# Rows of the first mixture gathered by token number, and grouped-query projections begun on half of the tokens

## Chip, cores and metric

The kernel runs on one core of one Trainium2 chip. The metric is the device time of one launch in microseconds (us); lower is better. TensorE (PE in the profile) multiplies matrices and turns tiles, VectorE (DVE), ScalarE (ACT) and GpSimd (POOL) do the elementwise work, and SyncE (SP) issues most of the DMA transfers; gathers and scatters by index are issued from POOL's queue.

## The reference

A two-layer decoder on x of 4 x 256 tokens x 256 channels. Each part normalises x and adds its result to x:

```python
x = x + L0_attn(layernorm(x))     # a linear-decay mixer
x = x + L0_xattn(layernorm(x))    # latent cross attention over 1601 context rows
x = x + L0_ffn(layernorm(x))      # the first mixture: top-1 of 8 experts, capacity 160
x = x + L1_attn(layernorm(x))     # grouped-query attention, 16 heads, 4 key/value heads
x = x + L1_xattn(layernorm(x))
x = x + L1_ffn(layernorm(x))      # the second mixture: top-2 of 16 experts, one shared
```

The first mixture, as far as it matters here:

```python
logits = tokens @ gate_weight.T                  # (1024, 8)
top1 = argmax(logits);  mask = one_hot(top1, E)
ranks = cumsum(mask, axis=0) - 1                 # place of a token in its expert's queue
mask = mask * (ranks < C)                        # C = 160 places per expert
dispatch = einsum('tec,th->ech', sec_mask, tokens)
expert_out = gelu(dispatch @ w1) @ w2            # per expert
out = einsum('tec,ech->th', combine_weights, expert_out)
```

And the start of the grouped-query attention:

```python
q, k, v = split(x @ w_qkv.T)                     # 16 + 4 + 4 heads of 128
q, k = layernorm(q) , layernorm(k)               # per head, with gain and bias
q = q * cos + rotate_half(q) * sin               # k likewise
```

## The kernel before

The 1024 tokens are 8 tiles of 128 rows; a half is four tiles, and X (128 x 8 x 256) stays in SBUF for the whole kernel. Every engine has one program, written out in the order in which it is to run. PSUM has eight banks, handed out in turn by `PsumBanks`: `begin` on TensorE claims the next bank for a key and waits until the engine named for it has emptied the key eight places back; `turn` transposes up to four tiles of 128 x 128 into one bank. `copy_out` on ScalarE or VectorE waits for a bank to be filled and copies it to SBUF. `link` makes an engine wait for its own last result.

**Normalising.** `normalise(k, g)` on VectorE adds the part before to X for the four tiles of half g, takes statistics, waits for ScalarE's square root (`deviations(k, g)`), and writes HN[k] with four operations (L1481), each counted in `hn_ready`. `turn_x(k)` on TensorE waits for `hn_ready` and turns a half into two banks, ("ht", k, g, 0) and ("ht", k, g, 1); one is copied out by ScalarE and one by VectorE into HT[k].

**The first mixture.** After the attention output product of token tiles 6 and 7 (`attended`), TensorE turns the second half of HN[2] (`turn_half(1)`), makes the router's logits (`logits0`, 16 matmuls of 8 columns a half), turns the weights of the next stage in between (`qkv_weights`, from a_nat, and then `awo`, from a_wo), and counts ranks with a triangle of ones (`rank0`). VectorE makes the slot number of each token, expert times 160 plus rank, into f_idx (L1728; a token without a place gets a number beyond the last slot), and then centres the weights a_wT of queries and keys (`centre`, four times a reduction, a small operation and a subtraction over 1280 columns, L1752 to L1754). Meanwhile:

- POOL clears f_xg, 128 x 10 x 256 (L2080), and f_yg (L2082). SP writes the cleared f_xg over all 1280 rows of xs0 in HBM (L2225).
- When f_idx is there, POOL scatters the eight tiles of HN[2] into the rows of xs0 (L2087, eight indirect transfers of 128 KB, `rows_sent`).
- When all eight have landed, SP loads xs0 back into f_xg, in five transfers of two slot tiles (L2230, `rows_back[g]`).
- TensorE turns group g (`slots_turned`, four transposes into a bank, key ("xg", g)); the even groups are copied out by ScalarE, the odd ones by VectorE. NEXT0 puts the groups before the experts: groups 0 and 1 before expert 0, group 2 before expert 2, 3 before 3, 4 before 5. `up0(e)` and `down0(e)` are the expert's two products, with Gelu on ScalarE between; VectorE copies the result (f_y), and SP stores it to ys0.
- When all results are stored, POOL gathers them back by token (f_yg, L2094, eight indirect transfers), and `normalise(3, g)` adds them to X (`result`, L1760).

SP issues its DMAs in the order of its program; before the tables of the next stage (a_cos, L2220, to a_gb) it waits for tile 7 of the attention output. Then come the zeros for xs0 and the experts' weights f_w1 and f_w2 (L2226, L2227, 2 MB each). In POOL's program the head tables of the next stage stand between the scatters and the gathers of results.

**The grouped-query projections.** After `turn_x(3)` all engines meet in `ended(3)`. Then TensorE runs units n: `qkv(n)` for token tile t = n // 6 and 512 columns g = n % 6 (four records of a matmul of 512 columns each in the trace); g = 5 is the values. For each of the 40 query and key units ScalarE squares (L1345), VectorE makes the rotated parts and sums the squares (`parts`, L1801 to L1804), ScalarE takes a square root (L1348) and scales four heads (L1336), POOL adds the parts (`rotated`, L2101) and the bias (`biased`, L2107), and TensorE turns the result (`qk_turn`), for unit n - 4 after unit n. POOL's order is rotated 0, 1, 2, biased 0, rotated 3, biased 1, and so on. The causal mask is loaded by SP after `ended(3)`.

The second mixture, at the end of the kernel, already fetches its rows by token number. It holds the operations that the change adds to the first, on twice as many places: VectorE, L1905 to L1923 (e_idx, e_q, e_one, e_A, e_B, e_ids); TensorE, `tile_tokens`.

## Time and profile before

| | us |
|---|---|
| median of the runs | 1380.8 (1380.19 to 1387.83, 3 runs) |
| the profiled execution | 1383.64, of which the span from first to last instruction 1381.8 |
| granted TensorE clock, mean | 0.952 of 2.4 GHz |
| TensorE busy | 1269.7 (92%) |
| VectorE busy | 869.0 (63%) |
| GpSimd busy | 823.2 (60%) |
| ScalarE busy | 632.4 (46%) |

Busy time is a share of the whole span; the kernel is a row of stages with different limits, so what an edit in one stage is worth has to be read in that stage. All times in the rows count from the start of the span. A clock of 1.00 is 2.4 GHz, 0.50 is 1.2 GHz. A row of a timeline merges neighbouring instructions of the same kind; the brackets at its end give the idle time before it and what ended it.

### The profile page before, as it was taken

The page shows a single profiled execution, that of the slowest core. Times are in us where ns is not written, and L with a number is a line of the kernel's source. Part 1 is how long each engine was busy: PE and PEld are TensorE (multiplying, and loading weights), DVE is VectorE, ACT ScalarE, POOL GpSimd, SP SyncE. Part 2 cuts the span into 40 slices and gives each one's busy share as a digit, 9 for nine tenths or more (in the row PEclk, how much of TensorE's full clock was granted, in tenths as well). Part 3 has the DMA queues.
Part 4 walks back from the last instruction along what each step waited for, and adds up shares of the span by engine and source line. Part 5 has one row for each costly group of instructions (what it writes and reads, how often), then busy time and mean ns, then how long its engine had stood idle before and what let it go on. Part 6 is the DMA issues. An engine that isn't in the chain of part 4 may idle for free.

```text
span 1381.8 us, 20338 instructions
## 1 busy us (share of the span) xinstructions
PE 1269.7 (92%) x7115; PEld 826.3 (60%) x7115; DVE 869.0 (63%) x1484; ACT 632.4 (46%) x1684; POOL 823.2 (60%) x747
## 2 busy tenths in 40 slices
PE   7999997999999999999999567998999999998792
PEld 4865554666666666666668553445776884557582
DVE  4756666677777777778865526675666113764543
ACT  3731123445544455444551315887666015881151
POOL 1267005799999999999993535887544003660444
PEclk9999997999999999999999688998999997998996
DMA  8501111000000000000004720000000105200263
GB/s 260 134 9 34 36 31 27 9 8 9 9 12 8 9 9 9 12 9 9 9 5 166 234 60 12 1 0 1 1 1 1 28 1 155 62 1 32 67 144 118
DMA packets 67532, 60.12 MB, mean 44 GB/s; under 512 B 19440, under 2 KB 64392, under 8 KB 66920
## 3 DMA queue, kind: packets, MB, share of 16 engines
q1 hardware_dynamic: 64408, 50.56, 13.1%
q0 software_dynamic: 3024, 8.26, 2.6%
q8 instruction: 58, 0.95, 0.3%
q14 instruction: 42, 0.34, 0.1%
HBM read 40.58 MB, written 9.83 MB: 36 GB/s over the span
## 4 chain that ended last, share of the span: by engine, by line
PE 79%; DVE 6%; ACT 5%; POOL 5%; issue 4%; DMA 1%; DVEq 0%; SPq 0%; POOLq 0%; ACTq 0%
PE PS L503 73%; PE PS L511 5%; ACT s_sc L1379 2%; POOL a_m L2107 2%; POOL a_m L2101 2%; DVE s_mx L1826 1%; ACT a_m L1336 1%; DVE pm L1599 1%; DVE HN L1481 1%; POOL slot_rows L2087 1%; PE PS L717 0%; POOL s_sc L2122 0%; PE PS L673 0%; PE PS L611 0%; DVE stats L1471 0%
## 5 line engine op out<-in xcount | busy, mean ns | idle before, releaser
L2047 POOL TENSOR_TENSOR PWS<-PWS 128x1024 f32<-128x1024 f32 x160 | 379.5, 2372 | 45.6 <-ACT PWS L1264 26.2
L1599 DVE TENSOR_REDUCE pm<-PS 128x2 f32<-128x1024 f32 x192 | 225.8, 1218 | 69.5 <-PE PS L503 69.1
L1264 ACT ACTIVATE PWS<-PS 128x512 f32<-128x512 f32 (+1 forms) x416 | 213.1, 600 | 78.5 <-PE PS L503 77.2
L503 PE MATMUL PS<-PWS,KVR 128*64 128x256 f32 (+1 forms) x1664 | 185.9, 380 | 0.0
L503 PE MATMUL PS<-QALL,KH 128*128 128x512 f32 (+1 forms) x416 | 182.9, 440 | 0.9 <-DVE QM L1623 0.9
L503 PE MATMUL PS<-QM,KL 68*128 68x512 f32 (+1 forms) x416 | 167.1, 402 | 0.0
L2122 POOL TENSOR_SCALAR s_sc<-s_sc,s_ri 128x128 f32<-128x128 f32 (+1 forms) x256 | 103.9, 425 | 99.5 <-DVE s_ri L1833 99.5
L503 PEld LDWEIGHTS PS<-PWS,KVR 128*64 128x64 f32 (+1 forms) x1664 | 121.1, 137 | 59.3 <-issue 0.9
L503 PEld LDWEIGHTS PS<-QALL,KH 128*128 128x128 f32 (+1 forms) x416 | 77.9, 187 | 76.9 <-ACT PWS L1264 57.2
L1379 ACT ACTIVATE s_sc<-PS,s_nb 128x128 f32<-128x128 f32 (+1 forms) x256 | 104.4, 431 | 4.9 <-DVE s_nb L1829 4.9
L1826 DVE TENSOR_REDUCE s_mx<-PS 128x2 f32<-128x512 f32 (+2 forms) x112 | 65.7, 611 | 52.0 <-PE PS L503 51.7
L503 PE MATMUL PS<-KH,QALL 64*128 64x512 f32 (+1 forms) x512 | 89.3, 408 | 7.0 <-DVE pm L1599 7.0
L503 PE MATMUL PS<-a_wT,HT 128*128 128x512 f32 x192 | 90.1, 602 | 0.7 <-ACTq L490 0.7
L1275 ACT ACTIVATE QALL<-CTX 128x256 fp32r<-128x256 f32 x32 | 13.3, 417 | 154.3 <-DVE CTX L1636 154.3
L503 PEld LDWEIGHTS PS<-QM,KL 68*128 68x128 f32 (+1 forms) x416 | 79.0, 190 | 6.2
L503 PEld LDWEIGHTS PS<-KH,QALL 64*128 64x128 f32 (+1 forms) x512 | 46.9, 189 | 43.6 <-issue 26.0
L503 PE MATMUL PS<-z_HTh,z_w 128*128 128x512 f32 x192 | 67.5, 420 | 2.4 <-DVEq L490 2.4
L2150 POOL DMA_INDIRECT e_x<-token_rows,e_ids x31 | 29.4, 949 | 64.4 <-DVE e_ids L1923 45.7
L1249 ACT ACTIVATE QALL<-PS 64x512 fp32r<-64x512 f32 x32 | 18.9, 592 | 106.4 <-PE PS L503 106.0
L2101 POOL TENSOR_TENSOR a_m<-a_m,a_m 128x512 f32<-128x512 f32 x40 | 50.8, 1271 | 27.0 <-DVE a_m L1803 27.0
L1502 DVE TENSOR_TENSOR X<-X,PS 128x256 f32<-128x256 f32 x40 | 16.7, 418 | 76.6 <-PE PS L503 76.6
L1367 ACT ACTIVATE s_pt<-PS 128x512 f32<-128x512 f32 x64 | 38.5, 602 | 50.1 <-PE PS L511 50.1
(319 smaller groups left out, 2516.9 us busy)
## 6 DMA issues: line engine op xcount, KB each, us to landing
QALL<-qlo SPq DMA_DIRECT2D x32, 128.0 KB, 2.4
QM<-QALL SPq DMA_DIRECT2D x64, 64.0 KB, 2.0
f_w<-in_L_ffn_w_dram SPq DMA_DIRECT2D x2, 2048.0 KB
tile_results<-e_y SPq DMA_DIRECT2D x31, 128.0 KB
a_nat<-in_L_attn_w_qkv_dram SPq DMA_DIRECT2D x1, 3072.0 KB, 13.4
x_wq<-in_L_xattn_Wq_dram SPq DMA_DIRECT2D x1, 2048.0 KB, 11.2
x_wo<-in_L_xattn_Wo_dram SPq DMA_DIRECT2D x2, 1024.0 KB, 6.8
a_wo<-in_L_attn_w_o_dram SPq DMA_DIRECT2D x1, 2048.0 KB, 17.8
```

The costliest lines, as they stand in the source:

```text
L503: return nc.tensor.matmul(o, a, b, start=start, stop=stop, **kw)
L511: last = nc.tensor.transpose(ps[0:w, c:c + r], a, ident[0:r, 0:r])
L1264: nc.scalar.activation(PW[c][0:rows, j * HALF:(j + 1) * HALF], st_bank("block", LT * u + lt)[0:rows, :], ACT.Exp).then_inc(p_ready, 1)
L1367: nc.scalar.activation(s_pt[:, m % 2, 0, :], ps, ACT.Copy).then_inc(emptied["act_turned"], 1)
L1379: ins = nc.scalar.activation(s_sc[:, k % 4, h, 0:nk], ps[:, j * nk:(j + 1) * nk], ACT.Exp, bias=s_nb[:, k % 3, h:h + 1], scale=scale, accu ...
L1599: V.tensor_reduce(pm[u % 2][:, :, i // 3, i % 3], src, AX, ALU.max).then_inc(nat_read, 1)
L1826: ins = V.tensor_reduce(s_mx[:, k % 3, i * per:(i + 1) * per], banks.bank(key)[:, 0:per * nk].rearrange("p (h k) -> p h k", h=per), AX, AL ...
L2047: G.tensor_tensor(ACC[:, :], PW[0][:, :] if i == 0 else ACC[:, :], PW[i + 1][:, :], ALU.add).then_inc(acc_step, 1)
L2101: G.tensor_tensor(a_m1[:, n % 6, :], a_m1[:, n % 6, :], a_m2[:, n % 2, :], ALU.add).then_inc(m_sum, 1)
L2107: G.tensor_tensor(m1, m1, a_bt[:, i, s, :].unsqueeze(1).to_broadcast([P, 4, P]), ALU.add).then_inc(qk_ready, 1)
L2122: ins = G.tensor_scalar(s_sc[:, n % 4, h, 0:nk], s_sc[:, n % 4, h, 0:nk], s_ri[:, n % 4, h:h + 1], 1.0, ALU.mult, ALU.mult)
L2150: G.indirect_dma_start(e_x[:, j % 8, :], None, xs1, IndirectOffsetOnAxis(ap=e_ids[:, j:j + 1], axis=0)).then_inc(tile_back[j % 8], 16)
```

## The change

1. **Rows by token number.** HN[2] is stored as it is, by two transfers of SP, one for each half (`rows_stored`); xs0 now has 1024 rows. The clear of f_xg, the zeros over xs0 and the eight scatters are gone. VectorE splits each slot number into place (modulo 128) and tile, makes one-hots of both (f_B; f_A holds the tile's one-hot times the token's number within its tile and times 128 times its tile), eight bf16 matmuls multiply them on TensorE (key "ids0", placed after four of the six turns of `qkv_weights(1)`), and VectorE adds the two parts to f_ids: the token of each slot. POOL gathers ten tiles of 128 rows by f_ids straight into f_xg; `rows_back[g]` counts two gathers. A slot without a token fetches token 0, whose result nobody reads.
2. **All five groups** ("xg", g) are copied out by ScalarE.
3. **Projections on half of the tokens.** TensorE turns only the first half before the projections, and the second after unit 4; `qkv` waits for the banks of its own half. The ended(3) of all engines is gone, and the later ones are renumbered. VectorE copies ("ht", 3, 0, 0) between its two normalisations; ScalarE copies both banks of the second half, after its work for unit 1. The mask load waits for the last of these copies.
4. On SP the store of the first half stands before the wait for tile 7, the store of the second, with a wait for its HN[2], before the loads of the tables; the constants f_c are a fourth load ahead of a_nat.

```diff
+        xs0 = nc.dram_tensor("token_rows_3", [B * T, C], F32, kind="Internal").ap()
+        f_B = at("f_B", 190720, [P, NT, P], BF16)
+        f_A = at("f_A", 57344, [P, NT, 2, TILES0], BF16)
@@ turn_x (TensorE)
-                        turn(("ht", k, g, kc), "act" if kc and k != 1 or (k, g) in ((0, 0), (5, 0)) else "dve",
+                        turn(("ht", k, g, kc), "act" if kc and k != 1 or (k, g) in ((0, 0), (3, 1), (5, 0)) else "dve",
@@ slots_turned (TensorE)
-                pe.wait_ge(rows_back[g], 16)
-                turn(("xg", g), "dve" if g % 2 else "act",
+                pe.wait_ge(rows_back[g], 32)
+                turn(("xg", g), "act",
@@ tensor
             rank0()
-            qkv_weights(1)
+            qkv_weights(1, range(0, 4))
+            pe.wait_ge(slot_onehot, 1)
+            ps = begin("ids0", "dve")
+            for t in range(NT):
+                last = mm(ps[:, 0:2 * TILES0], f_B[:, t, :], f_A[:, t, :, :].rearrange("p s j -> p (s j)"), t == 0, t == NT - 1)
+            last.then_inc(filled, 1)
+            qkv_weights(1, range(4, 6))
...
-            turn_x(3)
-            ended(pe, 3)
+            turn_x(3, (0,))
...
             def qkv(n):
                 t, g = n // 6, n % 6
+                if g == 0 and t % 4 == 0:
+                    for kc in range(KC):
+                        pe.wait_ge(*banks.emptied(("ht", 3, t // 4, kc)))
...
                 qkv(n)
                 t, g = n // 6, n % 6
+                if n == 4:
+                    turn_x(3, (1,))
                 if g < 5 and 5 * t + g >= 4:
                     qk_turn(5 * t + g - 4)
@@ scalar
-            for g in range(2):
-                deviations(3, g)
-            ht_out(3)
-            ended(act, 3)
+            deviations(3, 0)
+            heads_out(3, 0, 1)
+            deviations(3, 1)
...
                     copy_out(("qkv", n // 5 - 1, 5), a_v[:, n // 5 - 1, :])
+                if n == 1:
+                    for kc in range(KC):
+                        heads_out(3, 1, kc)
                 if n >= 4:
                     qk_out(n - 4)
@@ vector
             V.tensor_copy(f_idx[:, :], f_slot[:, :]).then_inc(slots_ready, 1)
+            dve.wait_ge(slots_ready, 1)
+            link(V.tensor_scalar(f_qu[:, :], f_idx[:, :], P - 1, None, ALU.bitwise_and))
+            link(V.tensor_copy(f_q[:, :], f_qu[:, :]))
+            link(V.tensor_tensor(f_jq[:, :], f_slot[:, :], f_q[:, :], ALU.subtract))
+            link(V.tensor_tensor(f_one[:, :, :], bcast(f_jq[:, :], TILES0), f_tiles.unsqueeze(1).to_broadcast([P, NT, TILES0]), ALU.is_equal))
+            V.tensor_scalar(f_A[:, :, 0, :], f_one[:, :, :], f_p, None, ALU.mult)
+            V.tensor_tensor(f_A[:, :, 1, :], f_one[:, :, :], bcast(f_high, TILES0), ALU.mult)
+            V.tensor_tensor(f_B[:, :, :], bcast(f_q[:, :], P), f_iota.unsqueeze(1).to_broadcast([P, NT, P]),
+                            ALU.is_equal).then_inc(slot_onehot, 1)
+            ps = banks.take("ids0", "dve")
+            dve.wait_ge(*banks.filled("ids0"))
+            V.tensor_reduce(f_idf[:, :], ps[:, 0:2 * TILES0].rearrange("p (s j) -> p j s", s=2), AX, ALU.add).then_inc(emptied["dve"], 1)
+            dve.wait_ge(*banks.emptied("ids0"))
+            V.tensor_copy(f_ids[:, :], f_idf[:, :]).then_inc(slot_ids, 1)
...
             normalise(3, 0, result)
+            copy_out(("ht", 3, 0, 0), HT[3][:, 0, 0:HALF])
             normalise(3, 1, result)
-            ht_out(3)
-            ended(dve, 3)
@@ gpsimd
-            G.memset(f_xg[:, :, :], 0.0)
             pool.drain().then_inc(slots_cleared, 1)
             link(G.memset(f_yg[:, :, :], 0.0))
             last_slot = G.to_reg(SLOTS0 - 1)
-            pool.wait_ge(slots_zeroed, 16)
-            pool.wait_ge(slots_ready, 1)
-            for t in range(NT):
-                G.indirect_dma_start(xs0, IndirectOffsetOnAxis(ap=f_idx[:, t:t + 1], axis=0), HN[2][:, t, :], None,
-                                     bounds_check=last_slot, oob_is_err=False).then_inc(rows_sent, 16)
+            pool.wait_ge(rows_sent, 32)
+            pool.wait_ge(slot_ids, 1)
+            for j in range(TILES0):
+                G.indirect_dma_start(f_xg[:, j, :], None, xs0, IndirectOffsetOnAxis(ap=f_ids[:, j:j + 1], axis=0)).then_inc(rows_back[j // 2], 16)
@@ sync
+            sp.dma_start(f_c[:, 0:209], tri_c[:, P:P + 209]).then_inc(moe0_loaded, 16)
...
+            rows_stored(0)
             sp.wait_ge(*banks.emptied(("xo", NT - 1)))
+            rows_stored(1)
...
-            sp.wait_ge(slots_cleared, 1)
-            sp.dma_start(xs0.rearrange("(j p) c -> p j c", p=P), f_xg[:, :, :]).then_inc(slots_zeroed, 16)
...
-            sp.wait_ge(rows_sent, 16 * NT)
-            for g in range(SLOTS0 // P // 2):
-                sp.dma_start(f_xg[:, 2 * g:2 * g + 2, :],
-                             xs0[2 * g * P:2 * (g + 1) * P, :].rearrange("(j p) c -> p j c", p=P)).then_inc(rows_back[g], 16)
...
-            sp.wait_ge(phase_ended, 4 * 3)
+            sp.wait_ge(*banks.emptied(("ht", 3, 1, 1)))
```

## Rows read from the trace of the kernel before

**Rows 1.** Windows by stage: length, busy time by engine, clock, DMA share, GB/s.
```profile
778.00:790.00 12.00, 0.03 (x1) 0.04 (x1) 6.64 (x7) 1.09 (x3) 9.42 (x13) 0.61 0.44 149
```

**Rows 2.** TensorE's timeline: start us, us, instruction, count, idle time before and releaser.
```profile
755.54 1.84 PE L503 MATMUL PS<-g_T,HT 128*128 128x8 f32 x16
...
761.51 1.09 PE L511 MATMUL PS<-ident,HN 128*128 128x128 f32 x8 [2.33 <-DVE HN L1481]
763.39 3.44 PE L503 MATMUL PS<-g_T,HT 128*128 128x8 f32 x16 [0.79 <-ACT HT L1145]
...
789.97 1.97 PE L511 MATMUL PS<-ident,f_xg 128*128 128x128 f32 x8 [11.98 <-DMA f_xg<-slot_rows]
...
796.96 0.60 PE L511 MATMUL PS<-ident,f_xg 128*128 128x128 f32 x4
...
830.62 1.97 PE L511 MATMUL PS<-ident,HN 128*128 128x128 f32 x8 [13.57 <-DVE HN L1481]
...
838.95 10.36 PE L503 MATMUL PS<-a_wT,HT 128*128 128x512 f32 x20 [0.72 <-ACTq L490]
851.02 0.66 PE L511 MATMUL PS<-ident,a_m 128*128 128x128 f32 x4 [1.72 <-POOL a_m L2107]
```

**Rows 3.** VectorE's timeline, first mixture and start of the projections.
```profile
757.48 3.98 DVE L1481 TENSOR_SCALAR HN<-X,mv,rstd 128x256 f32<-128x256 f32 x4
...
771.27 0.17 DVE L1728 CAST f_idx<-f_slot 128x8 uint32<-128x8 f32 x1
...
773.60 1.49 DVE L1754 TENSOR_TENSOR a_wT<-a_wT,a_mu 128x1280 f32<-128x1280 f32 x1
...
834.82 1.38 DVE L1481 TENSOR_SCALAR HN<-X,mv,rstd 128x256 f32<-128x256 f32 x4
...
847.06 0.66 DVE L1801 TENSOR_TENSOR a_m<-PS,a_gc 128x512 f32<-128x512 f32 x1
```

**Rows 4.** GpSimd's timeline, first mixture: the two clears and three of eight scatters.
```profile
756.49 2.23 POOL L2080 MEMSET f_xg<- 128x2560 f32 x1
758.86 1.80 POOL L2082 MEMSET f_yg<- 128x2048 f32 x1 [0.15 <-issue]
772.33 1.20 POOL L2087 DMA_INDIRECT slot_rows<-HN,f_idx  x1 [11.67 <-DVE f_idx L1728]
773.84 2.12 POOL L2087 DMA_INDIRECT slot_rows<-HN,f_idx  x1 [0.31 <-issue]
...
777.55 1.64 POOL L2087 DMA_INDIRECT slot_rows<-HN,f_idx  x1 [0.30 <-issue]
```

**Rows 5.** SP's timeline: tables, expert weights, and the rows' way back.
```profile
756.19 0.34 SPq L2220 DMA_DIRECT2D a_cos<-in_cos_c_dram  x1
...
759.87 0.72 SPq L2226 DMA_DIRECT2D f_w<-in_L_ffn_w_dram  x1
...
787.15 2.41 SPq L2230 DMA_DIRECT2D f_xg<-slot_rows  x5
```

**Rows 6.** Windows of 1 us, first, one within and last of the full DMA stream (columns as above).
```profile
763.00:764.00 1.00, 0.61 (x4) 0.64 (x4) 0.52 (x4) 0.29 (x1) 0.00 (x0) 0.76 0.84 295
...
769.00:770.00 1.00, 1.00 (x6) 1.00 (x7) 0.01 (x1) 0.98 (x2) 0.00 (x0) 0.50 1.09 349
...
779.00:780.00 1.00, 0.00 (x0) 0.00 (x0) 0.96 (x2) 0.10 (x1) 0.70 (x2) 1.00 0.84 306
```

**Rows 7.** VectorE's timeline in the second mixture: from slots to one-hots.
```profile
1282.34 0.17 DVE L1905 CAST e_idx<-e_slot 128x16 uint32<-128x16 f32 x1
...
1284.77 2.35 DVE L1913 TENSOR_TENSOR e_B<-e_q,e_c 128x1024 bf16<-128x1024 f32 x2
```

**Rows 8.** The tile f_yg: its gathers (ns min/median/max, first and last start), and their landing.
```profile
L2094 POOL DMA_INDIRECT f_yg<-slot_results,f_idx x8: 994/998/1072, 820.6 to 829.8; - x8
...
DMA to landing us min/median/max: 2.8/2.8/2.9
```

**Rows 9.** ScalarE's timeline: the first square of the projections.
```profile
842.53 0.60 ACT L1345 ACTIVATE a_sq<-PS 128x512 f32<-128x512 f32 x1 [3.68 <-PE PS L503]
```

More of the change, by code:

```diff
@@ L330, in decoder @@
         slots_cleared = sem("slot_rows_cleared")
-        slots_zeroed = sem("slot_rows_zeroed")
         slots_ready = sem("token_slots_ready")
-        rows_sent = sem("token_rows_sent")
+        slot_onehot = sem("first_slot_one_hots_ready")
+        slot_ids = sem("slot_tokens_ready")
+        rows_sent = sem("token_rows_stored_3")
         res_added = sem("token_results_added")
@@ L915, in _ @@
                 qk_turn(n)
-            ended(pe, 4)
+            ended(pe, 3)
             def softmax_units(tag, units, turnable, score, use):
@@ L988, in _ @@
             turn_x(4)
-            ended(pe, 5)
+            ended(pe, 4)
             for ct in range(KC):
@@ L1128, in _ @@
                 shared_down(t)
-            ended(pe, 6)
+            ended(pe, 5)
         @block.scalar
@@ L1353, in _ @@
                     copy_out(("qkv", n // 5 - 1, 5), a_v[:, n // 5 - 1, :])
+                if n == 1:
+                    for kc in range(KC):
+                        heads_out(3, 1, kc)
                 if n >= 4:
                     qk_out(n - 4)
-            ended(act, 4)
+            ended(act, 3)
             def softmax_units(tag, units, base_n, scale):
@@ L1396, in _ @@
             turned_norm(4)
-            ended(act, 5)
+            ended(act, 4)
             for ct in range(KC):
@@ L1444, in _ @@
             nc.scalar.activation(f_e[:, :, :], f_e[:, :, :], ACT.Exp).then_inc(e_exp, 1)
-            ended(act, 6)
+            ended(act, 5)
         @block.vector
@@ L1767, in _ @@
             for e in range(E0 + 1):
-                for g in NEXT0[e] if e < E0 else ():
-                    if g % 2:
-                        copy_out(("xg", g), f_xT[:, :, 2 * g * P:2 * (g + 1) * P], lambda ps: ps.rearrange("p (k s) -> p k s", k=KC))
                 if e >= 1:
@@ L1816, in _ @@
             V.tensor_copy(s_identb[:, :], ident[:, :]).then_inc(mask_set, 1)
-            ended(dve, 4)
+            ended(dve, 3)
             def softmax_units(tag, units, base_n, scale, after):
@@ L1847, in _ @@
             turned_norm(4, added("ao"))
-            ended(dve, 5)
+            ended(dve, 4)
             def y_after(n, unit):
@@ L1960, in _ @@
                 V.scalar_tensor_tensor(X[:, t, :], e_yg[:, t, 1, :], e_w[:, 1, t:t + 1], X[:, t, :], ALU.mult, ALU.add).then_inc(x_final, 1)
-            ended(dve, 6)
+            ended(dve, 5)
         @block.gpsimd
@@ L2095, in _ @@
                                      bounds_check=last_slot, oob_is_err=False).then_inc(res_back[t], 16)
-            ended(pool, 3)
             def rotated(n):
@@ L2113, in _ @@
                     biased(n - 2)
-            ended(pool, 4)
+            ended(pool, 3)
             G.memset(y_v[:, :, :, :, :], 0.0).then_inc(v_cleared, 1)
@@ L2137, in _ @@
             masked_keys(0)
-            ended(pool, 5)
+            ended(pool, 4)
             masked_keys(1)
@@ L2155, in _ @@
                     G.indirect_dma_start(e_yg[:, t, k, :], None, ys1, IndirectOffsetOnAxis(ap=e_idx[:, k * NT + t:k * NT + t + 1], axis=0)).then_inc(both_back[t], 16)
-            ended(pool, 6)
+            ended(pool, 5)
         @block.sync
```

23 lines of the change are left out of this document (17 added, 6 removed).

## Prediction, made before the changed kernel was run

> **What bounds the kernel now.** I read the windows by stage first, then the chain of waits from 750 to 860 us, and then the timeline of each engine around the two places that the change touches. The page has TensorE busy for 92% of the span, but from 778 to 790 us it does nothing (0.03 of 12 us) [rows 1]. There it waits 11.98 us for rows of the first mixture [rows 2], and the timelines say why: slot numbers stand at 771.44 (771.27 + 0.17), eight scatters through POOL's queue follow, then a copy back from HBM at 787.15 [rows 3 to 5]. A second gap of 13.57 us ends at 830.62, when the first half of the tokens is normalised, and the second half follows before the projections start at 838.95 [rows 2]. So two places carry the change: the way of the rows (771 to 790), and the start of the projections (830 to 851). What lies between them moves along.
>
> **The head start from the removed clear.** The clear of f_xg (2.23 us) and that of f_yg (1.80) run on POOL from 756.49 to 760.66 [rows 4]. The four HN operations of VectorE between them take 3.98 us, the same four at 834.82 only 1.38 [rows 3]: the ones that meet a clear end with it. Without the f_xg clear, the f_yg clear runs from about 756.7 to 758.5, the first HN operation ends with it, three more of about 0.35 follow, and the second half is ready at about 759.7 in place of 761.46. That is 1.8 us off the chain. TensorE then idles 0.5 us instead of 2.33 before the transposes at 761.51. The 16 router matmuls on that half take 3.44 us, the 16 on the first half took 1.84 [rows 2]; the granted clock falls inside 763 to 764 [rows 6], after that gap. The new matmuls run from about 761.6 to 763.5, with hardly a gap before them, so I take them at 2.4 GHz and 1.84 us: 1.6 us more. Both ends: 0 and 1.6. Slot numbers: 771.44 - 1.8 - 1.6 = 768.0.
>
> **The new work between slots and rows.** The before shows the same operations in its second mixture: from e_idx at 1282.34 to the end of the two e_B operations at 1287.12 (1284.77 + 2.35) [rows 7]. Here there are half the slots: the small ones 0.21 each with their link, the 80-element one-hots 0.2 to 0.27, one e_B of 1.22 in place of two. Three times 0.21, 0.27, 0.15, 0.2 and 1.22 are 2.5 us. Eight matmuls, TensorE's answer and the semaphore: 0.6. Reduction and cast: two small operations like the cast to e_idx (0.17) with their links, 0.46 [rows 7]. POOL's start after the last value took 0.89 in the before (771.44 to 772.33). First gather at 768.0 + 2.5 + 0.6 + 0.46 + 0.89 = 772.5, nearly where the first scatter stands now, since the head start pays for the one-hots.
>
> TensorE has to be free for those eight matmuls at 770.6: before them lie rank0, which ended at about 770.0 and now ends 3.4 earlier, and 16 transposes (0.2 each at the slow clock), so it is free by 769.8. Behind them it has 40 transposes left (1.97 us for 8 cold ones: at most 10 us), done by 781, before the rows come. ACT copies them out meanwhile. VectorE's centring of a_wT (4 times about 3.3 us) starts only after the ids, at 772, and ends at 785; its next work, the copy of the first f_y, comes at about 788. Hidden.
>
> **Rows by gather.** TensorE's first expert needs xg 0 and, because both groups are turned before it, xg 1: four gathers. Alone a gather takes 0.99 us (f_yg) plus 0.3 between two, and lands 2.8 us after its start [rows 8]. But the issues at 773.84 and 777.55 took 2.12 and 1.64 us [rows 4]; each met a TENSOR_TENSOR of the centring, which runs from 773.60 for 1.49 us and again every 3.25 us [rows 3]. The centring is behind the ids by nearly as much as the gathers, so the pattern stays: in the before the fourth issue ended 779.19 - 772.33 = 6.9 us after the first began. So the fourth ends at 779.4 and lands 1.8 us later, at 781.2. Unheld, the fourth would start 3.9 us after the first and land at 779.2. Against 789.97 that is 8.8 us. The first group was turned meanwhile: of the 8 transposes only 4 (0.9 us of the 1.97) are left. Together 9.7 us up to the end of the experts. The gathers for groups 2 to 4 come every 2.6 to 3.4 us, TensorE asks for the first of them at 796.96, 7 us after its start [rows 2], and for the others about 3 and 9 us after that: hidden. That ACT now copies all five groups costs nothing: an expert takes TensorE about 3 us, and ACT spends on it one copy of 0.6 at most and the Gelu. Head tables start 3 us later on POOL, and have ten to spare.
>
> The Trainium skill says otherwise on one point: SBUF — State Buffer, "Who interferes with whom", says that a VectorE tensor_tensor with both inputs in SBUF locks out GpSimd's reads, and infers that generating descriptors for a GpSimd DMA, which needs the write side, is not held up. The trace of this case shows issues prolonged by about the rest of the TENSOR_TENSOR. By the page the fourth gather would land 2.0 us earlier, and the sum would be 1367.6.
>
> **The expert weights** must be there too. SP now waits for the second half before it issues a_cos, where it began at 756.19, so f_w1 goes from 759.87 [rows 5] to 759.7 + 0.5 + 3.2 = 763.4, 3.5 us later. The DMA engines are full from 763 to 779.8 [rows 6], by the tiles' sizes with 1.3 MB of zeros and 4.2 MB of weights and six scatters; at 349 KB per us the zeros cost 3.8 us, and they are gone. The stream ends about where it did, near 780; the first expert asks at 782.1. Hidden, with 2 us to spare. The store of the first 0.5 MB at 746 delays a_wo by 1.5 us, and TensorE asks for it only at 757.24; bound 0 to 1.
>
> **Projections.** Shown in the times of the before, everything after TensorE's experts unchanged up to 830.62: 8 transposes (1.97) and the ACT copy (0.7) give qkv(0) at 833.3 instead of 838.95, 5.6 us early. But this is not the gain. The second half's transposes stand behind five units on TensorE, and ACT copies them out (heads_out(3, 1)) after square 1 and before square 2. Five units took 10.36 us in the before [rows 2], with a cold start; from 833.3 that is 843.6, a little less because the transposes have begun to warm it: 843.3. Then 8 transposes (1.0, half of the cold 1.97), the ACT copy and square 2 (0.6 each, [rows 9]): VectorE starts its third unit at 845.6 instead of 847.06 [rows 3]. From there to the first qk_turn at 851.02 [rows 2] the sequence is the old one (POOL adds in the order r2, b0). Gain 1.5 us. VectorE's copy of ht 3,0,0 before normalise(3, 1) delays the second half by about 1.8 us to 838.0: not late, TensorE turns at 843. Ends: 3.2 us if all five units run at 2.4 GHz, 0 if the cold part doubles. The 119 us after that have POOL and the PSUM order as before; I price them at 0. The barrier, the drain and the mask load: 0, nothing waits on them last.
>
> **Sum.** 9.7 + 1.5 = 11.2 us. Against the profiled span 1381.8 (its run 1383.6) that is 1370.6; against the median 1380.8 of the runs, 1369.6. One per cent, about what a measurement of this kernel can tell, is 13.8 us.
>
> **Rivals.**
> 1. *The gathers are not held, and the projections start warm*: 2.0 + 1.7 more, 1365.9, over 1% faster. For it: the phase of the centring to the gathers can slip by a microsecond. Against: two of the first four issues met it. The page's inference above is the first half of this rival.
> 2. *Rows or weights late in the full DMA stream*: the gathers run at 772 to 779 under the stream of weights. The worst a queue can do is to serve them after it: 780 + 0.5 MB at 349 = 781.5, and the later landing for the last 1.8: 783.3; with a cold router (1.6) and no gain at the projections: 11.2 - 2.1 - 1.6 - 1.5 = 6.0, so 1374.8.
> 3. *Gathers far slower than the f_yg ones* (the other side): the four rows' transfers come from HBM while weights stream; no row shows that. Price: each us of landing is one us. At 11.2 us, a landing at 792.4, it turns slower than before; over 1% from 806. The stream is over at 780, so this needs a new cause.
> 4. *The overlap gives its full 5 us* (ACT not behind TensorE): 1366.1. Against: the order in the code.
>
> DMA: Bandwidth & Descriptors ("Queues, rings and completion order") of the Trainium skill says each DMA engine takes turns between queues by packets. No row of the before shows a gather's landing under load; by that rule the gathers would come before the stream's end, as in my sum.
>
> **Numbers.** Forecast 0.60; rival 1 0.10, rival 2 0.18, rival 3 0.04, rival 4 0.08. Predicted 1369.6. The range takes in rivals 1, 2 and 4 and a little of the runs' own spread: 1364.5 to 1376. Over 1% faster (below 1367.0) needs rival 1 or 4: 0.18. Slower by over 1%: half of rival 3, 0.02. Within: 0.80.
>
> **What would show it.** Second half of HN 2 ready 1.8 us earlier, router matmuls of 1.8 us, first gather near 772.5, first expert matmul near 782, experts' end near 807; then in the first projections an ACT gap before the third square, ended by TensorE's transposes. It would be wrong if the clock falls all the same, if TensorE waits for weights, or if the tile period in the projections is no longer 14.1 us.

## Result and profile after

| | before | changed |
|---|---|---|
| median of 20 runs, us | 1381.25 (1375.34 to 1392.67) | 1374.33 (1366.67 to 1388.71) |
| ratio, with its 95% interval | | 0.9937 [0.9919, 0.9955] |
| span of the profiled execution | 1381.8 | 1379.6 |
| mean granted clock | 0.952 | 0.954 |

The ratio is 8.7 us less (6.2 to 11.2), the medians differ by 6.9. The ratio leaves out three slow executions of the changed kernel (1387.65 to 1388.71) and none of the kernel before, so it flatters the change a little: over all 20 of each the means differ by 6.6 us. Forecast were 1369.6 in a range of 1364.5 to 1376 and no change over 1%. Range and class came out, but the time lies near that of the second rival (1374.8), and partly by its mechanism, as the rows show.

At the end of stage 2 the changed kernel's profile is 0.25 us ahead (the last addition to X on VectorE at 755.49, before 755.74), in code that the change does not touch. That is taken off below. VectorE and GpSimd, from the removed clear to the gathers, answer to [rows 3, 4]:

```profile
756.45 1.81 POOL L2114 MEMSET f_yg<- 128x2048 f32 x1 [0.15 <-issue]
...
757.23 2.14 DVE L1504 TENSOR_SCALAR HN<-X,mv,rstd 128x256 f32<-128x256 f32 x4
...
770.96 0.17 DVE L1765 CAST f_ids<-f_idf 128x10 uint32<-128x10 f32 x1
...
773.29 1.49 DVE L1791 TENSOR_TENSOR a_wT<-a_wT,a_mu 128x1280 f32<-128x1280 f32 x1
774.82 1.49 DVE L1789 TENSOR_REDUCE a_mu<-a_wT 128x10 f32<-128x1280 f32 x1
```

HN takes 2.14 us in place of 3.98, and the token numbers stand at 771.13. The chain of waits then runs from them to the rows (start, us, what):

```profile
772.00 1.17 POOL f_xg L2119
...
773.48 2.13 POOL f_xg L2119
...
775.91 0.95 POOL f_xg L2119
...
777.16 6.37 DMA f_xg<-token_rows,f_ids
```

The first gather stands at 772.00 (forecast 772.5). The second starts beside the TENSOR_TENSOR at 773.29 and is held to 2.13 us; the third starts beside the TENSOR_REDUCE at 774.82 and takes 0.95. The fourth, the last that the first expert needs, lands 6.37 us after its start, at 783.54; the forecast was 781.2. SP's timeline and, in a second fence, windows of 1 us say what was in the DMA engines [rows 5, 6]:

```profile
763.35 0.44 SPq L2263 DMA_DIRECT2D f_w<-in_L_ffn_w_dram  x1
763.83 6.42 SPq L2264 DMA_DIRECT2D f_w<-in_L_ffn_w_dram  x1
```

```profile
763.00:764.00 1.00, 1.00 (x8) 1.00 (x9) 0.64 (x4) 0.01 (x1) 0.00 (x0) 0.66 0.19 56
...
766.00:767.00 1.00, 1.00 (x7) 1.00 (x7) 0.55 (x3) 0.99 (x2) 0.00 (x0) 0.50 0.18 51
...
769.00:770.00 1.00, 0.76 (x4) 0.35 (x2) 1.00 (x3) 0.75 (x2) 0.00 (x0) 0.50 1.00 354
...
780.00:781.00 1.00, 0.39 (x2) 0.39 (x3) 1.00 (x1) 0.00 (x0) 0.69 (x2) 0.69 1.00 329
781.00:782.00 1.00, 0.73 (x4) 0.33 (x2) 0.97 (x2) 0.23 (x1) 1.00 (x1) 0.50 0.55 192
```

The weights were issued at 763.35 as forecast (763.4), but the engines moved 51 to 56 KB a us until 767 and were full only later, up to 781: the stream ends between 781 and 782, some 1.7 us behind that of before. The four gathers are issued under it, and the fourth lands 2 us after its end. TensorE's timeline, which answers to [rows 2]:

```profile
759.42 1.09 PE L523 MATMUL PS<-ident,HN 128*128 128x128 f32 x8 [0.49 <-DVE HN L1504]
761.30 1.92 PE L515 MATMUL PS<-g_T,HT 128*128 128x8 f32 x16 [0.79 <-ACT HT L1167]
...
780.61 1.12 PE L523 MATMUL PS<-ident,f_xg 128*128 128x128 f32 x4 [5.48 <-DMA f_xg<-token_rows,f_ids]
783.58 1.11 PE L523 MATMUL PS<-ident,f_xg 128*128 128x128 f32 x4 [1.85 <-DMA f_xg<-token_rows,f_ids]
784.49 3.68 PE L515 MATMUL PS<-f_xT,f_w 128*128 128x160 f32 x16
...
823.30 1.97 PE L523 MATMUL PS<-ident,HN 128*128 128x128 f32 x8 [13.48 <-DVE HN L1504]
826.00 11.60 PE L515 MATMUL PS<-a_wT,HT 128*128 128x512 f32 x20 [0.73 <-issue]
837.44 1.04 PE L523 MATMUL PS<-ident,HN 128*128 128x128 f32 x8
843.72 1.12 PE L523 MATMUL PS<-ident,a_m 128*128 128x128 f32 x4 [5.25 <-POOL a_m L2137]
844.63 5.61 PE L515 MATMUL PS<-a_wT,HT 128*128 128x512 f32 x8
850.07 0.60 PE L523 MATMUL PS<-ident,a_m 128*128 128x128 f32 x4
```

The wait of 11.98 us has become two of 5.48 and 1.85, with transposes at half speed between them. The first half of the normalised tokens is turned at 823.30 in place of 830.62. Then the gain shrinks: before the first turn of queries TensorE stands for 5.25 us (1.72 before), and the eight matmuls behind it take 5.61 us in place of 3.60, so that the second turn of queries follows the first after 6.35 us in place of 3.93. The rows of the kernel before for that:

```profile
851.52 3.60 PE L503 MATMUL PS<-a_wT,HT 128*128 128x512 f32 x8
854.95 0.60 PE L511 MATMUL PS<-ident,a_m 128*128 128x128 f32 x4
```

ScalarE and VectorE of the changed kernel show what it waited for [rows 3, 9]:

```profile
838.07 1.08 ACT L1167 ACTIVATE HT<-PS 128x512 f32<-128x512 f32 x2 [4.80 <-PE PS L523]
839.04 0.60 ACT L1365 ACTIVATE a_sq<-PS 128x512 f32<-128x512 f32 x1
...
839.74 0.69 DVE L1834 TENSOR_TENSOR a_m<-PS,a_gc 128x512 f32<-128x512 f32 x1 [4.52 <-issue]
```

ScalarE idles 4.80 us for the transposes of the second half, copies them, and only then squares the third unit. VectorE starts that unit at 839.74, which is 16.44 us after the turn at 823.30; before it was 847.06 - 830.62 = 16.44 too.

### The profile page after: what moved, and what is told of

It reads as the page before. It is cut to its first block, busy times and chain, and to the rows that moved or that the text cites. A ratio compares the mean times of both kernels' runs of the same rounds, so it can differ in the third digit from the quotient of the medians.

```text
span 1379.6 us, 20358 instructions
## 1 busy us (share of the span) xinstructions
PE 1272.7 (92%) x7123; PEld 826.8 (60%) x7123; DVE 868.2 (63%) x1490; ACT 634.6 (46%) x1687; POOL 824.0 (60%) x748
## 4 chain that ended last, share of the span: by engine, by line
PE 79%; DVE 6%; ACT 5%; POOL 4%; issue 4%; DMA 1%; DVEq 0%; SPq 0%; POOLq 0%; ACTq 0%
PE PS L515 73%; PE PS L523 5%; ACT s_sc L1402 2%; POOL a_m L2137 2%; POOL a_m L2131 2%; DVE s_mx L1859 1%; ACT a_m L1356 1%; DVE pm L1622 1%; DVE HN L1504 0%; PE PS L729 0%; DMA f_xg<-token_rows,f_ids 0%; POOL s_sc L2152 0%; PE PS L685 0%; POOL f_xg L2119 0%; PE PS L623 0%
## 5 line engine op out<-in xcount | busy, mean ns | idle before, releaser
L1622 DVE TENSOR_REDUCE pm<-PS 128x2 f32<-128x1024 f32 x192 | 225.8, 1218 | 69.3 <-PE PS L515 68.7
L515 PE MATMUL PS<-a_wT,HT 128*128 128x512 f32 x192 | 93.4, 620 | 0.7 <-issue 0.7
```

The source lines that it names most:

```text
L515: return nc.tensor.matmul(o, a, b, start=start, stop=stop, **kw)
L1622: V.tensor_reduce(pm[u % 2][:, :, i // 3, i % 3], src, AX, ALU.max).then_inc(nat_read, 1)
```

## How the profiles are compared

Executions of one kernel spread over up to 22 us (1366.67 to 1388.71), so I split every profiled span at four rows: the last addition to X before HN 2 is normalised (the end of stage 2); **R**, from there to the turn of the first half of HN 3 on TensorE (first mixture); **P**, from that turn to the second turn of queries (start of the projections); **L**, from the addition to the turn of HN 4's second half (it holds R, P and the rest of the attention); **Y**, from there to the router matmuls of the second mixture (latent attention); and the rest. For the kernel before, the rows give L = 1141.62 - 755.74 = 385.88 and Y = 1263.35 - 1141.62 = 121.73:

```profile
755.74 0.42 DVE L1502 TENSOR_TENSOR X<-X,PS 128x256 f32<-128x256 f32 x1 [2.35 <-PE PS L503]
...
1141.62 1.27 PE L511 MATMUL PS<-ident,HN 128*128 128x128 f32 x8 [2.34 <-DVE HN L1481]
...
1263.35 1.93 PE L503 MATMUL PS<-m_rT,HT 128*128 128x16 f32 x16 [1.40 <-ACT HT L1145]
```

All values are differences of such rows. "chip" numbers the three groups of kernels that ran on one chip.

| kernel | chip | addition at | R | P | L | Y | rest |
|---|---|---|---|---|---|---|---|
| before | - | 755.7 | 74.9 | 24.3 | 385.9 | 121.7 | 118.4 |
| changed | - | 755.5 | 67.8 | 26.8 | 380.5 | 123.4 | 120.2 |
| rows_only | 1st | 757.2 | 68.2 | 24.6 | 378.7 | 124.1 | 118.7 |
| half_only | 1st | 757.8 | 74.8 | 27.2 | 388.3 | 120.7 | 119.8 |
| turn_early | 1st | 758.2 | 68.2 | 20.7 | 374.8 | 130.1 | 120.2 |
| tables_first | 1st | 755.4 | 64.7 | 26.5 | 377.3 | 126.4 | 118.6 |
| warm_y | 2nd | 752.7 | 68.3 | 25.1 | 379.3 | 115.9 | 109.9 |
| centre_late | 2nd | 751.4 | 64.1 | 27.0 | 377.0 | 115.3 | 108.6 |
| both | 2nd | 758.3 | 64.8 | 20.6 | 371.3 | 120.6 | 109.8 |
| all_four | 2nd | 754.1 | 62.7 | 20.3 | 368.8 | 115.9 | 109.9 |
| after_again | 3rd | 752.2 | 68.7 | 24.7 | 379.4 | 117.6 | 118.8 |
| tables_first_again | 3rd | 754.7 | 63.6 | 25.9 | 375.4 | 120.6 | 119.9 |
| centre_late_again | 3rd | 753.5 | 64.0 | 27.1 | 377.0 | 115.3 | 118.7 |
| before_warm | 3rd | 755.4 | 74.9 | 24.3 | 386.0 | 118.4 | 118.4 |

In L the kernel before and before_warm, whose code is the same up to there, agree within 0.1 us; the changed kernel, warm_y and after_again within 1.3, tables_first and its repeat within 1.8. So L reads an edit to somewhat under two microseconds, where Y alone moves by 15 us between kernels whose code there is the same. Theories A and C in the texts below are the two readings of the trace above: A, the place of the second half's turn costs what the early start brings; C, the rows wait in the stream of weights, which starts too late.

## Experiments

**rows_only: the projections' part undone.** All of the change but the half-way start:

```
-            turn_x(3, (0,))
+            turn_x(3)
+            ended(pe, 3)
...
-                if n == 4:
-                    turn_x(3, (1,))
```

> The changed kernel with its projections undone: rows by token number stay, but both halves are turned before the projections, with the meeting of all engines, as in the kernel before. Theory A (in the changed kernel the projections on half of the tokens cost about 2.4 us, because TensorE idles 5.25 us before its first turn of a query unit and then runs the next two units at the slow clock): experts end where they do in the changed kernel, near 809.8; the first turn of a query unit comes about 7 us before 851.0, TensorE idles 1.7 us before it, and the second follows 3.9 us after the first as in the kernel before. Time about 7 us under the kernel before, 2 us under the changed kernel. Rival B (the half-way start gains the 1.5 us that were predicted, or nothing): 0 to 1.5 us above the changed kernel.

Measured: 1377.37, ratio 0.996 [0.9935, 0.9985], which is 5.5 us below the kernel before (forecast 7) and not below the changed kernel (forecast 2). L is 7.2 us below the kernel before, P is 0.3 above it. TensorE's timeline:

```profile
846.03 0.66 PE L523 MATMUL PS<-ident,a_m 128*128 128x128 f32 x4 [1.69 <-POOL a_m L2133]
846.53 3.60 PE L515 MATMUL PS<-a_wT,HT 128*128 128x512 f32 x8
849.97 0.60 PE L523 MATMUL PS<-ident,a_m 128*128 128x128 f32 x4
```

The wait is 1.69 us again, the units behind it take 3.60. In L the rows alone bring at least as much as both parts together (7.2 against 5.3, 6.5 and 6.6), within what L can tell. The whole time does not separate them: the intervals overlap.

**half_only: only the half-way projections, on the kernel before.** The same lines the other way round.

> The kernel before with only the projections on half of the tokens. Theory A: first turn of a query unit near 851, as in the kernel before, but the second 6.4 us after it instead of 3.9; about 2.4 us slower than the kernel before. Rival B: 0 to 1.5 us faster.

Measured: 1387.9, ratio 1.0029 [0.9999, 1.0058], L 2.4 us above the kernel before, as forecast, and P 2.8 above:

```profile
853.36 1.11 PE L511 MATMUL PS<-ident,a_m 128*128 128x128 f32 x4 [5.24 <-POOL a_m L2111]
854.26 5.74 PE L503 MATMUL PS<-a_wT,HT 128*128 128x512 f32 x8
859.84 0.60 PE L511 MATMUL PS<-ident,a_m 128*128 128x128 f32 x4
```

The same wait and the same slow units as in the changed kernel, without its gathers. So this part of the change gains nothing by itself; in its profile it loses 2.8 us of P.

**turn_early: the second half turned behind the second unit.**

```
-                if n == 4:
+                if n == 1:
                     turn_x(3, (1,))
```

> The changed kernel, with the second half turned on TensorE after unit 1 instead of after unit 4. Theory A: ScalarE's wait before its third square shrinks from 4.8 us to about 1; third unit of VectorE near 836 instead of 839.7, first turn of a query unit near 840 instead of 843.7, TensorE idles under 2.5 us before it and stays at the fast clock, so the second turn comes 3.9 us later instead of 6.4. In all about 6 us under the changed kernel. Rival B (the clock falls in any case, or something else holds the second turn): 3.8 us under the changed kernel, the second turn still 6.4 us after the first.

Measured: 1372.65, ratio 0.994 [0.9916, 0.9963]. TensorE's timeline:

```profile
835.63 1.04 PE L523 MATMUL PS<-ident,HN 128*128 128x128 f32 x8
836.50 5.32 PE L515 MATMUL PS<-a_wT,HT 128*128 128x512 f32 x12
843.09 0.66 PE L523 MATMUL PS<-ident,a_m 128*128 128x128 f32 x4 [1.27 <-POOL a_m L2137]
843.58 3.60 PE L515 MATMUL PS<-a_wT,HT 128*128 128x512 f32 x8
```

The wait is 1.27 us, P is 6.1 us shorter than in the changed kernel (4.0 than in its repeat) and 3.7 below the kernel before, L 11.1 below it. Theory A holds: it is the place of the turn, and the early start is worth 3.7 us when nothing stands in its way. In the whole time the 6 us that were expected do not show, the ratio is that of the changed kernel (0.994 and 0.9937); the profiled execution was the slowest of ten (1384.99), and its Y is 130.1.

**tables_first: the head tables ahead of SP's wait for the second half.**

```
-            rows_stored(1)
             ...
+            rows_stored(1)
```

(the line moves from ahead of the loads of a_cos, a_sin and a_gb to behind them, ahead of f_w)

> The changed kernel, with the six table loads issued by SP ahead of its wait for the second half, so that the expert weights go out 3.4 us earlier. Theory C (the fourth gather lands 6.4 us after its start instead of 3.5 because the stream of weights fills the DMA engines until 781.5): the stream ends near 778, the fourth gather lands 3.5 to 4.5 us after its start, near 781, and the first expert and all behind it come 2 to 2.7 us earlier. Rival D (ten gathers of 1 KB rows are slow by themselves, or in each other's way): landing stays at 6.4 us, no gain.

Measured: 1372.46, ratio 0.9942 [0.9918, 0.9967], so nothing of the expected 2 to 2.7 us in the whole time; R is 3.1 us below the changed kernel. SP's timeline, a window of the DMA engines at the end of the stream, then the chain of waits:

```profile
759.75 0.51 SPq L2263 DMA_DIRECT2D f_w<-in_L_ffn_w_dram  x1
```

```profile
776.00:777.00 1.00, 0.00 (x0) 0.00 (x0) 0.93 (x3) 0.17 (x1) 0.79 (x1) 1.00 0.75 244
```

```profile
777.10 3.40 DMA f_xg<-token_rows,f_ids
...
780.53 1.12 PE PS L523 x4
```

The weights are issued 3.6 us earlier and the stream ends before 777, and the fourth gather, started at the same time (777.10, changed 777.16), lands after 3.40 us in place of 6.37. Its issue ends at 778.80, so it lands 1.7 us after that, the 1.8 of the forecast. The repeat and the run of both edits below show the same (3.43 and 3.41 us from start to landing). Theory C holds.

**centre_late: no TENSOR_TENSOR beside the first gathers.** On top of tables_first, the centring of a_wT is moved:

```
-            for kc in range(KC):
-                for _ in centre(kc):
-                    pass
+            dve.wait_ge(rows_back[1], 32)
+            centring = (0 for kc in range(KC) for _ in centre(kc))
+            for _ in range(2):
+                next(centring)
             for e in range(E0 + 1):
+                if e in (2, 3):
+                    next(centring)
...
```

> The changed kernel with the head tables issued ahead of SP's wait (weights 3.4 us earlier, as in the run before), and the centring of a_wT on VectorE moved behind the landing of the first four gathers: two of its four steps then, the other two after the copies of experts 0 and 1. So no TENSOR_TENSOR runs beside the first four gathers. Theory H (a TENSOR_TENSOR holds the issue of a gather): all four issues take 0.95 to 0.99 us, the fourth starts 3.8 us after the first in place of 5.1, and TensorE turns the second pair 1.3 us earlier relative to the first gather (7.2 us after its start in place of 8.5). Rival (what holds them is the DMA queue under the weights' stream): two of four issues take 1.6 us and more all the same. Whole time: 0 to 1.5 us below the kernel with the tables first (1372.5).

Measured: 1353.98, ratio 0.9857 [0.9823, 0.9891]. The chain of waits:

```profile
769.32 0.95 POOL f_xg L2124
...
770.57 0.95 POOL f_xg L2124
...
771.82 3.65 DMA f_xg<-token_rows,f_ids
```

The second to fourth issue take 0.95 us each; in tables_first they took 2.13, 0.95 and 1.70. The windows show the DMA engines as full as in the changed kernel (348 and 375 KB in the microseconds from 769 and from 772). Theory H holds: it was the TENSOR_TENSOR, and not the full DMA engines. This run takes all of the centring away; that the reductions of the same size do not hold an issue is read from the changed kernel, where the gather beside one took 0.95 us. The fourth gather starts 3.97 us after the first (5.16 in the changed kernel), and the first expert begins 8.3 us after the first gather (9.5 with the tables alone, 12.5 in the changed kernel). But R is 64.1 against 64.7 (64.0 and 63.6 in the repeats), and L the same within two microseconds: the edit gains nothing that can be seen. The whole gained far more than that; the repeat below shows that this was not the edit.

**warm_y: repeated mask matmuls in the latent attention.** The changed kernel, with values unchanged:

```
                 for ps in both:
-                    mask(ps, st, 2)
+                    for _ in range(3 if n in (3, 4) else 1):
+                        mask(ps, st, 2)
```

> The changed kernel, and in the latent attention's units 3 and 4 each causal mask matmul (128x256, 0.19 us at 2.4 GHz) is issued three times over in place of once, each writing the same values anew: 8 more of them, 1.5 us of TensorE's work, put where TensorE waited 0.85 and 1.03 us for POOL's softmax of the first two units. Question: does that wait bring the clock down for the 22 to 24 us that follow it (granted 0.53, 0.50, 0.69 from 1152 to 1176 in the changed kernel)? Theory D (the wait just before does it): the clock stays at 1.00 through the stage, which shrinks from 123.4 us (from the turn of HN 4's second half to the router matmuls) to 110 to 114, the whole by 8 to 12 us. Rival (the low activity of the whole start of the stage, 32-row score matmuls and gaps of 2.35 and 0.72 us before, does it): the clock falls all the same, stage 122 to 125, whole time within 2 us of the changed kernel.

Measured: 1361.64, ratio 0.9913 [0.9884, 0.9942], Y 115.9, with the clock below 1.00 for about 4 us near its start and at 1.00 from there on (changed 123.4, forecast 110 to 114). The ratio is 3.3 us below that of the changed kernel, where 8 to 12 were expected; the intervals overlap, and the two ran on different chips. That is a miss.

**both: tables first and the early turn.** The two edits above together.

> The changed kernel with the tables issued ahead of SP's wait and the second half of the tokens turned behind the second unit of the projections instead of the fifth. Theories A and C together: each alone brought 3.1 and 5.8 us locally against the changed kernel, up to the second turn of queries, so the second turn comes 13.4 us earlier than in the kernel before, at the same start. If local gains reach the end: 1374.3 - 8.9 = 1365.4. If the later stages give part of them back by their clock, as the single runs suggest (each moved the whole by 2 us only): 1369 to 1372.

Measured: 1360.22, ratio 0.9894 [0.9868, 0.9921]. L is 371.3, 14.6 us below the kernel before. R (64.8) is that of tables_first, P (20.6) that of turn_early: they add up. By the ratio, against the kernel before on the same chip, the whole is 14.6 us less too. Expected were 1365.4, or 1369 to 1372 if later stages gave gains back; 1360.22 is below both, on a chip where other stretches are shorter too (see the repeats).

**all_four: tables, early turn, late centring, repeated masks.**

> The changed kernel with all of it: tables first, centring behind the first gathers, second half turned behind the second unit, and the repeated mask matmuls in the latent attention. If everything holds and adds up: 1374.3 - 3.1 - 1.3 - 5.8 - 10 = 1354. If only the clock of the latent attention cannot be held: 1364 to 1370.

Measured: 1350.37 (expected 1354), ratio 0.9839 [0.9808, 0.987], the fastest version: 22 us below the kernel before on that chip, its interval below that of the changed kernel. L is 368.8, 17.1 us below the kernel before. On the same chip warm_y has the same code in the last stages and the change as it was: 1361.64, 11.3 us more, and L says 379.3 - 368.8 = 10.5. So in this pair the local gain reaches the end. In another pair on that chip it does not: the kernel with tables and early turn has an L 5.7 us shorter than centre_late and yet takes 6.2 us longer (1360.22 and 1353.98, and their runs do not overlap). In the profiles it reaches the addition 6.9 us later and its Y is 5.3 longer, in stretches that neither edit touches.

**after_again, centre_late_again, tables_first_again, before_warm.** The last is warm_y's edit on the kernel before; the others are repeats, on a third chip.

> The changed kernel once more, beside the three others of this call. The runs of the last call gained more against the kernel before (0.986 to 0.989) than the same local gains would give, and the stretch behind the latent attention was 110 us long in place of 118 to 120. If a faster chip or a lucky clock is behind that: the ratio stays near 0.9937 and the profile shows which stretch differs. If the change is worth more than the first figure said: ratio 0.990 or less.

> The kernel with the tables first and the centring behind the first gathers, once more. By the local sums up to the projections it should be 1.2 us (8.3 against 9.5 us from the first gather to the first expert) below the next kernel; the first figures (0.9857 against 0.9942) say 11.7. If the local sum is all: 0.998 to 1.000 of the next kernel. If the rest was the chance of the latent attention's clock: a profile of this one with a slow stretch of 16 us or more there shows up, or the next one's without.

> The kernel with only the tables first, beside the two above: 3.0 us below the changed kernel by the landing of the fourth gather, ratio to it 0.998; first gather to first expert 9.5 us against 12.5.

> The kernel BEFORE with only the repeated mask matmuls of the latent attention (units 3 and 4, 8 more matmuls of 0.19 us, same values). Theory D: the clock of the stretch from 1150 to 1180 us stays at 1.00, the stage takes 114 to 117 us in place of 121.7, the whole 5 to 7 us less (ratio 0.995 to 0.996). Rival: the stage's clock is a matter of chance, ratio 0.999 to 1.001, and the profile shows a stretch at 0.50 of 8 us or more in the stage.

| | median | ratio |
|---|---|---|
| after_again | 1372.43 | 0.9948 [0.9915, 0.9981] |
| centre_late_again | 1371.24 | 0.9944 [0.9907, 0.9982] |
| tables_first_again | 1371.17 | 0.9927 [0.99, 0.9955] |
| before_warm | 1380.47 | 0.9988 [0.9964, 1.0012] |

The change's first figure stands (0.9937 and 0.9948, though both intervals are wide). The 0.9857 of centre_late does not: on the third chip it is 0.9944, beside 0.9927 for the tables alone. The table of spans shows where the second chip differed: its rest is 108.6 to 109.9 us in four profiles out of four, 118.4 to 120.2 in the ten others. There is no profile of the kernel before from that chip (its runs had a median of 1373.74 there, 1380.4 to 1381.3 elsewhere), so how much of that the ratios of that chip carry stays open. What can be compared on it are its four kernels with each other.

before_warm's Y is 118.4 (121.7 before). One window of 8 us of before, then of before_warm, in the latent attention (the clock is the third number from the end):

```profile
1160.00:1168.00 8.00, 7.71 (x43) 4.00 (x46) 4.39 (x13) 5.14 (x23) 4.62 (x12) 0.50 0.46 117
```

```profile
1160.00:1168.00 8.00, 7.06 (x69) 3.94 (x68) 5.36 (x19) 7.33 (x32) 5.90 (x15) 1.00 0.44 112
```

In the three profiles with the repeated masks the clock stays at 1.00 for 75 us and more from unit 3 on. Of the eleven without, eight have a stretch of over 10 us below 1.00 there, three (after_again and both of centre_late) a short one. centre_late and its repeat have the shortest Y of all, 115.3, without them. So the masks may keep the clock up, but three profiles with them against three others that do without is thin, and that they do is not shown. The gain that theory D promised is refuted: 0.995 to 0.996 was expected of the whole time of before_warm, and its interval begins at 0.9964.

## Why the prediction was right, and where its steps failed

**The clear, the router's clock, the one-hots: right.** From 761.51 to 759.42 is 2.1 us, less the 0.25 of start: 1.84 (forecast 1.8). The router took 1.92 us (1.84), and the first gather came at 772.00 (772.5). But the reason given for the router's fast clock, that hardly a gap stands before it, is not borne out: the clock still fell inside 763 to 764, as before. In the fourteen profiles it fell 7.7 to 9.4 us after the last addition to X, 7.7, 7.8 and 8.5 where TensorE had idled 2.3 us before the transposes and 7.8 to 9.4 where it had idled 0.5. The router was fast because it ran 1.8 us earlier and ended 7.7 us after the addition, just ahead of the fall. That its time came out as forecast owes something to luck.

**The hold of the gathers: right.** Issues of 2.13 and 1.69 us beside TENSOR_TENSORs of the centring, the fourth ending at about 778.9 (forecast 779.4). The Trainium skill (SBUF — State Buffer, "Who interferes with whom") infers that descriptor generation is not held up by such an operation. The runs of centre_late, its repeat and all_four, with the operation elsewhere under the same stream of weights, have those issues at 0.95 us. Here the measurement decides, and it was the hold.

**The landing: a term of 1.8 us that measured 4.7.** The forecast took the 1.8 us after the end of the issue from the f_yg gathers [rows 8], although by its own account the weights would still stream until about 780. Measured: 783.54 less 778.85, the issue's end, is 4.7. Two steps failed: that a gather under the stream lands as one with the DMA engines free, and "The stream ends about where it did, near 780", where it ended 1.7 us later. The windows say why it did. The engines were full 4 to 5 us later than before and not 3.5 (they stood nearly idle from the issue at 763.35 to 767; before, from 759.87 to 763). And they moved 5.04 MB from 763 to 782, where before they moved 5.99 MB from 763 to 780: 0.95 MB less and not the 1.3 MB of zeros, since more gathers than scatters fall into the stream. The second rival named this case at 783.3. In tables_first the same gather took 1.7 us behind its issue's end. The Trainium skill's rule of turns by packets (DMA: Bandwidth & Descriptors, "Queues, rings and completion order") is neither refuted nor enough here: the first pair did land under the stream, by 780.57, but 5.0 us after the end of its second issue at 775.60, and the fourth gather landed after the stream's end and not before it.

With the turns at half speed (1.11 us for four, after idle times of 5.48 and 1.85 us), the first part gained 74.9 - 67.8 = 7.1 us by R, 6.1 and 6.6 in the two other profiles of the same code. Forecast were 9.7.

**The projections: the wrong sign.** Forecast was a gain of 1.5 us, up to the first turn of queries by "the sequence is the old one", and nothing for what follows ("I price them at 0"). Both terms failed. The five units were to be a little faster than before; they took 11.60 us (10.36), the clock at 0.50 to 0.57 from 826 to 832. They follow the wait of 13.5 us with one turn in between and not two, but that alone does not settle it: with this order the five units took 10.24 to 11.87 us in eight profiles, with both turns first 10.36 to 10.67 in three. The 11.60 us brought the third unit of VectorE to 16.44 us after the first turn, exactly the old distance: gain 0. The eight profiles have the first turn of queries from 1.3 us earlier to 0.3 us later than the old distance of 20.40 from the turn of HN 3, so the 1.5 was nearly met in one of them. The term priced at 0 failed in all eight. The sequence behind the first turn was the old one for VectorE and GpSimd but not for TensorE. Before, it went straight from its five units to a wait of 1.72 us; now its work is finished 3.5 us earlier relative to that turn and it stands 5.25 us. The windows of the changed kernel show what follows:

```profile
841.00:844.00 3.00, 0.28 (x2) 0.28 (x3) 2.93 (x9) 2.76 (x9) 2.83 (x3) 0.64 0.00 0
844.00:847.00 3.00, 3.00 (x7) 1.64 (x7) 1.78 (x5) 1.58 (x5) 3.00 (x3) 0.50 0.00 0
847.00:850.00 3.00, 3.00 (x6) 1.20 (x5) 0.00 (x0) 0.00 (x0) 1.57 (x2) 0.72 0.00 0
```

The clock falls to 1.2 GHz in the wait, and the next two units take 5.61 us, 2.0 more (4.97 to 5.74 in the eight profiles). P is longer by 2.4 us than before; in the seven other profiles with this order it is longer by 0.4 (after_again, where the five units took 10.24 us) to 2.8 (half_only).

**The sum again.** 11.2 forecast, less 2.6 in the first mixture and 3.9 (1.5 and 2.4) in the projections, is 4.7; the second turn of queries shows 854.95 - 850.07 - 0.25 = 4.6. L shows 5.3, 6.5 and 6.6 in three profiles, the whole 8.7 (6.6 over all executions) and 7.2 by its ratios, with intervals that reach down to 6.2 and 2.6. So about half of the 11.2 us came, and the range held by the room it gave to the second rival, and by 1.7 us only. The class held too: the gain is below 1%. The forecast time lay 2.9 us below the 1372.5 that the ratio gives (0.9937 of 1381.25), 4.7 below the median. The profiled span fell by 2.2 us only, since Y and the rest were 3.4 us longer in that execution; in all profiles these two differ by more than that with the same code.

The doubt that later stages give a local gain back by their clock came from the first group of runs, where turn_early and tables_first had Y of 130.1 and 126.4. The later ones do not bear it out: both, all_four and centre_late have larger gains in L, and Y of 115 to 121.

## What to carry to other kernels

When a step is moved ahead of a shared engine's old work, follow each engine through the new order separately: the engine that is bound can stay at its old distance, and one that finishes early stands, and here paid again in its clock. Here moving one line (the turn behind unit 2 in place of 5) decided between 0.4 to 2.8 us lost and 3.7 to 4.1 gained. The landing of a small gather has to be priced by what else the DMA engines carry at that time, and a large load that must be out of its way has to be issued earlier, not only made smaller. And where executions of the same code spread by over 1%, cut the span at rows ahead of and behind the edit: profiles of the same code agreed within 0.1 to 1.8 us there. That tells what an edit does in its stage; whether it reaches the whole time has to be measured beside it, on the same chip.

## What the runs showed of the hardware

- An indirect gather's issue takes 0.95 us alone (the first of a row of them 1.17), and 1.69 to 2.13 when a TENSOR_TENSOR of 1.49 us (128x1280, both inputs in SBUF) runs on VectorE; a wait for the landing of the first gathers ahead of that work removed it. A TENSOR_REDUCE of 1.49 us over the same tile did not prolong it (0.95).
- Under the stream of weights a gather of 128 rows landed 4.1 to 5.0 us after the end of its issue (second and fourth of the changed kernel 5.0 and 4.7, second of centre_late 4.5 and of its repeat 4.1), 2.7 where the stream ended between (fourth of centre_late), 1.7 with the stream over (fourth of tables_first).
- The latent attention took 115.3 to 130.1 us, with the granted clock below 2.4 GHz for about 4 us of it in the shortest and 44 in the longest, in code that is the same but for the masks.
- The rest took 108.6 to 109.9 us on one chip and 118.4 to 120.2 elsewhere. In nine of the ten slower profiles TensorE stops for 2.4 to 3.9 us before one transposition in the second mixture, for nothing that the profile shows; in the four of that chip it does not. In the changed kernel:

```profile
1298.56 0.33 PE L523 MATMUL PS<-ident,e_h 128*128 128x128 f32 x1 [2.50 <-issue]
```

What that stop is, and whether it accounts for the 9 us, no run here tells.
